# A graph kernel: where in a group its rows and keys are turned, and in what order TensorE and ScalarE take products, turns and counts

## The reference, cut to what matters

```
h = relu(layernorm(x))
m = relu(concat(h[src], edge_attr) @ w1a + b1a) @ w1b + b1b      # one message per edge, 96 wide
agg = segment_sum(m, dst) / max(count, 1)
x = x + (relu(concat(h, agg) @ w2a + b2a) @ w2b + b2b)
f = f0 = relu(layernorm(x))
repeat 10 times:
    f = 0.9 * segment_sum((f * src_norm)[src], dst) * dst_norm + 0.1 * f0
out = x + f
```

## Time and profile before

| what | value |
|---|---|
| median of 3 executions (lowest, highest) | 7052.78 us (7047.1, 7060.38) |
| the profiled execution's own time | 7054.22 us |
| its span | 7052.7 us |
| busy share of the span | PE 80%, PEld 53%, DVE 61%, ACT 10%, POOL 24% |
| mean granted TensorE clock | 0.862 |

### The profile page before, as it was taken

The page is one execution under the profiler, slowest core; times in us unless marked ns, Lnnn a source line. Parts: engine busy times, 40 slices in busy tenths (PEclk is TensorE's granted clock), DMA queues, the critical chain, the costliest instruction groups (busy, mean ns, idle before and its releaser), DMA issues. The chain is left out here.

```text
span 7052.7 us, 211605 instructions
## 1 busy us (share of the span) xinstructions
PE 5638.9 (80%) x85008; PEld 3706.2 (53%) x85008; DVE 4287.4 (61%) x12668; ACT 713.1 (10%) x1695; POOL 1693.6 (24%) x1739
## 2 busy tenths in 40 slices
PE   1455565655555557589999999999999999999998
PEld 1355454544454446446565565656555565656564
DVE  7455555555555557766656666666656666666665
ACT  0122222222222223000000000000000000000000
POOL 5555555555555552500000000000000000000000
PEclk9766666666667667799999999999999999999999
DMA  4322222222222222145555555555555555555554
GB/s 118 76 75 76 75 75 75 75 71 78 73 79 72 75 75 90 37 186 192 200 190 200 190 200 200 190 200 190 200 191 199 191 202 202 187 203 191 199 197 170
DMA packets 442865, 1016.62 MB, mean 144 GB/s; under 512 B 253162, under 2 KB 371914, under 8 KB 387354
## 3 DMA queue, kind: packets, MB, share of 16 engines
q1 hardware_dynamic: 386938, 968.76, 38.8%
q0 software_dynamic: 54944, 33.96, 2.6%
HBM read 838.78 MB, written 176.58 MB: 144 GB/s over the span
## 5 line engine op out<-in xcount | busy, mean ns | idle before, releaser
L1866 PE MATMUL banks_fast<-count_units_fast,feature_parts_fast 128*32 128x512 fp8e3 x70608 | 3826.2, 379 | 31.6 <-DVE count_units_fast L1761 27.0
L1866 PEld LDWEIGHTS banks_fast<-count_units_fast,feature_parts_fast 128*32 128x32 bf16 x70608 | 2154.4, 97 | 1680.2 <-issue 37.4
L1760 DVE TENSOR_SCALAR count_units_fast<-packed_ring_fast 128x512 int32<-128x512 int32 x2949 | 1257.0, 426 | 1427.4 <-PE banks_fast L1866 1396.9
L144 POOL DMA_INDIRECT rows_fast<-row_table,idx_fast x1456 | 1408.6, 967 | 1034.7 <-ACT count_stage_fast L1257 615.7
L1761 DVE TENSOR_SCALAR count_units_fast<-packed_ring_fast 128x512 int32<-128x512 int32 x2949 | 1238.8, 420 | 0.0
L1351 PE MATMUL banks_fast<-w1a_b1a_fast,turn_fast 49*128 49x96 f32 x3136 | 404.4, 399 | 905.1 <-ACT turn_fast L1262 561.4
L1223 DVE TENSOR_SCALAR window_place_hot_fast<-iota_wide_fast,local_keys_fast,target_weight_fast 128x196 bf16<-128x196 f16 x3136 | 939.3, 345 | 0.0
L1351 PEld LDWEIGHTS banks_fast<-w1a_b1a_fast,turn_fast 49*128 49x128 f32 x3136 | 319.6, 281 | 1015.8 <-issue 633.5
L1316 PE MATMUL banks_fast<-window_place_hot_fast,window_src_hot_fast 128*128 128x196 bf16 x3136 | 747.1, 335 | 29.5 <-DVE window_place_hot_fast L1223 25.9
L1322 PE MATMUL banks_fast<-window_place_hot_fast,window_src_hot_fast 128*128 128x196 bf16 x3136 | 728.7, 328 | 6.1 <-issue 6.0
L1219 DVE TENSOR_TENSOR window_src_hot_fast<-iota_by_windows_fast,window_keys_fast 128x1024 bf16<-128x1024 bf16 x392 | 269.6, 688 | 499.1 <-remote 364.1
(11 more groups left out here) (282 smaller groups left out, 1646.7 us busy)
## 6 DMA issues: line engine op xcount, KB each, us to landing
packed_ring_fast<-edge_counts SPq DMA_DIRECT2D x422, 1792.0 KB, 7.0
edge_counts<-count_stage_fast SPq DMA_DIRECT2D x100, 784.0 KB
running_sums<-run_sums_fast SPq DMA_DIRECT2D x100, 768.0 KB
rows_fast<-row_table,idx_fast POOLq DMA_INDIRECT x1456
rows_fast<-attrs_padded SPq DMA_DIRECT2D x98, 128.0 KB
attrs_padded<-in_edge_attr SPq DMA_DIRECT2D x1, 12500.0 KB
rows_fast<-row_table,src_ends_fast POOLq DMA_INDIRECT x112
row_table<-h_nodes_fast SPq DMA_DIRECT2D x1, 1568.0 KB, 5.2
```

Source lines behind the costliest of these rows:

```text
L144: pool.indirect_dma_start(out=self.rows[:, r, c, 0:DN], out_offset=None, in_=b.dram.table, in_offset=bass.IndirectOffsetOnAxis(ap=idx[:, c ...
L1760: nc.vector.tensor_scalar(to[..., 0:P // 8], of, NIBBLES, None, ALU.bitwise_and)
L1866: last = nc.tensor.matmul(b.banks[at:at + DN, SWEEP[m % 2], 0:COLS], parts[:, side, j, k * DN:(k + 1) * DN], of_strip.bitcast(FP8), start= ...
```

## The change

On TensorE the order becomes M0 T1 c0 to c3, M1 T2 c4 to c7, M2 T3 c8 to c11, M3, T0 of the next group, c12 to c15; the very first T0 stands ahead of the loop. On ScalarE it becomes R0 T1 C0 C1, R1 T2 C2 C3, R2 T3 C4 C5, R3, T0 of the next group, C6 C7. The keys of the next pair are turned before M1 of the pair's second group instead of before M3, and ScalarE copies them to SBUF (`kept_keys`) between R1 and the copy of T2; VectorE reads that copy and waits for it in place of R3. The last of the seven passes of the loop is written out behind it on both engines. SyncE's and GpSimd's code is unchanged, and so is the number of matmuls; ScalarE has 50 copies more.

```diff
@@ buffers @@
+        kept_keys = sb("kept_keys", [P, 2 * LW])
+        keys_kept = sem("keys_kept")
...
-        KEYS_AT = 384
+        KEYS_AT, KEYS_TURN = 384, 1
@@ VectorE, pass over the keys of a pair (s == 0) @@
-                        dve.wait_ge(keys_turned, k + 1)
-                        dve.wait_ge(mix_read, g * Q + 1)
+                        dve.wait_ge(keys_kept, k + 1)
                         dve.wait_ge(hot, (SLOTS + g) * WG)
...
-                        part_keys = b.banks[:, M_BANK, KEYS_AT:KEYS_AT + LW]
+                        part_keys = kept_keys[:, 0:LW]
...
-                        nc.vector.scalar_tensor_tensor(out=local[:, :], in0=b.banks[:, M_BANK, KEYS_AT + LW:KEYS_AT + 2 * LW],
+                        nc.vector.scalar_tensor_tensor(out=local[:, :], in0=kept_keys[:, LW:2 * LW],
@@ ScalarE @@
+            def keep_turned(n, slot):
+                act.wait_ge(turned, n + (SLOTS * Q + 1))
+                nc.scalar.copy(turn[:, slot, :], b.banks[:, T_BANK, 0:2 * P]).then_inc(turn_read, 1)
+            def keep_keys(k):
+                act.wait_ge(keys_turned, k + 1)
+                nc.scalar.copy(kept_keys[:, :], b.banks[:, M_BANK, KEYS_AT:KEYS_AT + 2 * LW]).then_inc(keys_kept, 1)
+            keep_keys(0)
+            keep_turned(0, 0)
+            def one_loop(i, last_loop):
...
-                    keep_turned(0)
                     act.wait_ge(sums_out[s], (k + 1) * 16)
                     act.sem_inc(passed, 1)
-                    relu_messages(0)
-                    act.wait_ge(counts_out[s], (k + 1) * 16)
-                    act.sem_inc(passed, 1)
                     for u in range(READS):
+                        q, at = divmod(u, QW // 4)
+                        if at == 0:
+                            relu_messages(q)
+                        if at == 0 and q == KEYS_TURN and s == SLOTS - 1:
+                            act.wait_ge(local_made, (k + 1) * KEY_STEPS)
+                            act.sem_inc(passed, 1)
+                            keep_keys(k + 1)
+                        if at == 0 and not (last_loop and t == BATCH - 1 and q == Q - 1):
+                            keep_turned(g * Q + q + 1, (q + 1) % 2)
+                        if u == 0:
+                            act.wait_ge(counts_out[s], (k + 1) * 16)
+                            act.sem_inc(passed, 1)
                         read_counts(u)
-                        q, at = divmod(u, QW // 4)
-                        if q < Q - 1 and at == 0:
-                            keep_turned(q + 1)
-                        if q < Q - 1 and at == 1:
-                            relu_messages(q + 1)
+            with act.Fori(0, n_loops - 1) as i:
+                one_loop(i, False)
+            one_loop(n_loops - 1, True)
@@ TensorE @@
+            def rows_in(r_rows, turns):
+                pe.wait_ge(gathered[r_rows], (turns + 1) * (G * 16))
+                pe.wait_ge(attrs_in[r_rows], (turns + 1) * 16)
+            def turn_rows(r_rows, q):
...
+            rows_in(0, 0)
+            turn_rows(0, 0)
+            def one_loop(i, last_loop):
...
-                    pe.wait_ge(gathered[r_rows], (turns + 1) * (G * 16))
-                    pe.wait_ge(attrs_in[r_rows], (turns + 1) * 16)
...
                         if q == 0 and s == 0:
-                            pe.wait_ge(local_made, pair * KEY_STEPS + 4)
-                        if q == Q - 1 and s == SLOTS - 1:
+                            pe.wait_ge(keys_kept, pair + 1)
+                        if q == KEYS_TURN + 1 and s == SLOTS - 1:
+                            pe.wait_ge(keys_kept, pair + 2)
+                        if q == KEYS_TURN and s == SLOTS - 1:
...
-                    turn_rows(0)
-                    mix(0)
                     for r in range(WG // 2):
+                        q, at = divmod(r, QW // 2)
+                        if at == 0:
+                            mix(q)
+                        if at == 0 and q < Q - 1:
+                            turn_rows(r_rows, q + 1)
+                        if at == 0 and q == Q - 1 and not (last_loop and t == BATCH - 1):
+                            rows_in((t + 1) % AHEAD_GROUPS, i * (BATCH // AHEAD_GROUPS) + (t + 1) // AHEAD_GROUPS)
+                            turn_rows((t + 1) % AHEAD_GROUPS, 0)
                         count(r)
-                        q, at = divmod(r, QW // 2)
-                        if q < Q - 1 and at == 1:
-                            turn_rows(q + 1)
-                        if q < Q - 1 and at == 2:
-                            mix(q + 1)
+            with pe.Fori(0, n_loops - 1) as i:
+                one_loop(i, False)
+            one_loop(n_loops - 1, True)
```

More of the change, by code:

```diff
@@ L1241, in _ @@
             act.sem_inc(count_read, SLOTS * READS)
-            with act.Fori(0, n_loops) as i:
+            def keep_turned(n, slot):
[7 more added lines that the diff above has]
+            def one_loop(i, last_loop):
                 nc.scalar.activation(first_act[:, :], b.zeros[:, 0:1], ACT.Relu).then_inc(first_done, 1)
@@ L1257, in read_counts @@
                         nc.scalar.copy(to, of).then_inc(count_read, 1)
-                    def keep_turned(q):
-                        act.wait_ge(turned, SLOTS * Q + g * Q + (q + 1))
-                        nc.scalar.copy(turn[:, q % 2, :], b.banks[:, T_BANK, 0:2 * P]).then_inc(turn_read, 1)
                     def relu_messages(q):
@@ L1301, in _ @@
             pe.sem_inc(turned, SLOTS * Q)
-            with pe.Fori(0, n_loops) as i:
+            def rows_in(r_rows, turns):
+                pe.wait_ge(gathered[r_rows], (turns + 1) * (G * 16))
+                pe.wait_ge(attrs_in[r_rows], (turns + 1) * 16)
+            def turn_rows(r_rows, q):
+                for k in range(QC // 2):
+                    c = q * QC + 2 * k
+                    last = nc.tensor.transpose(b.banks[:, T_BANK, k * P:(k + 1) * P],
+                                               rows[:, r_rows, c:c + 2, :].rearrange("p c d -> p (c d)"), b.ident[:, :])
+                last.then_inc(turned, 1)
+            rows_in(0, 0)
+            turn_rows(0, 0)
+            def one_loop(i, last_loop):
                 for t in range(BATCH):
-                    g, pair, s, r_rows, turns = (i * BATCH + t, i * PAIRS_A_LOOP + t // SLOTS, t % SLOTS, t % AHEAD_GROUPS,
-                                                 i * (BATCH // AHEAD_GROUPS) + t // AHEAD_GROUPS)
+                    g, pair, s, r_rows = i * BATCH + t, i * PAIRS_A_LOOP + t // SLOTS, t % SLOTS, t % AHEAD_GROUPS
                     def count(r):
```

## The result

| | before | after |
|---|---|---|
| median of 17 executions each on one chip (lowest, highest) | 7058.65 us (7042.45, 7070.84) | 7034.3 us (7020.29, 7051.65) |
| ratio, 95% interval | | 0.9969 [0.996, 0.9977] |
| profiled execution, its span | 7054.22, 7052.7 us | 7043.64, 7041.5 us |
| mean granted clock | 0.862 | 0.887 |

Faster by 24 us, where 115 were forecast. The time lies in the range (6780 to 7100) and far from the predicted 6940. Two things have to be read: the stage, and what lies behind it.

What follows compares the result with a forecast made beforehand. GpSimd's chain was taken to set the group: 20.5 us floor plus 6.8 us waiting for ScalarE's copies of counts, 27.3. 7054 - 110 (turns ahead) - 5 (last groups) = 6939, say 6940 us; range 6780 to 7100.

Steps and rivals of the forecast that it cites:

- What bounds the kernel: Gather stage: GpSimd's chain sets the 27.3 us group, 20.5 its own floor and 6.8 waiting for ScalarE's copies of counts.
- Turns a quarter ahead, counts in order: TensorE's lead in the gather stage: 1.61 GpSimd stops a group for 2.0, 1.2 us a group over 91 groups, -110 us.
- If T2's late signal arrives before the stop: Optimistic end in the gather stage: M2 and T3 run too, C6 and C7 come in, giving 12.5 DMAs a stop.
- The trickle: TensorE's late signals while gathers are under way, estimated to pass one by one at 0.7 to 1.5 us a signal.
- 8 to 12.5 bounds: Gather DMAs GpSimd issues per stop under the new order; with the ends, 7070 (keys included) and 6857 us.
- The middle, 10.25: DMAs a stop taken between the bounds: 16.5 / 10.25 = 1.61 stops a group, the basis of -110 us.
- Last pass written out: Last loop pass on TensorE and ScalarE: the same instructions in the same number, so 0.
- Signals prompt: Rival: signals are prompt, gathers slow the stage another way; only round trips go, 0.8 x 98 = -77, 6977 us; chance 0.05.
- Keys: Earlier key turns, VectorE's gain worth 0; 50 new ScalarE copies free, or +21 us if all are on the chain.
- ScalarE's order: Rival "slower": C1 and C0 queue behind R and a turn's copy, 0.8 us x 91 = +71, 7125 us; chance 0.19.
- Last groups: Last seven groups, which gather nothing: a turn's round trip, 0.8 us a group, is covered by four counts, -5 us.

## Why the prediction was wrong

**What bounds the kernel: right.** GpSimd's chain sets the group. Its floor of 20.5 us was met within 0.1 where nothing stopped it (20.4), and removing the gathers took 12 us a group off. The late signals are real, and they come at the stops.

**Turns a quarter ahead, counts in order (forecast -110): the failed step.** "If T2's late signal arrives before the stop ... M2 and T3 run too": mostly it does not arrive. The trickle, an estimate of 0.7 to 1.5 us a signal from one place in the earlier trace rows, is slower: nothing came in the 6.73 us before R1, and in the long run of gathers above signals came some 10 and 20 us late. So 8 and 9 DMAs became the usual run, the bottom of the 8 to 12.5 bounds, with some of 10 to 13. The middle, 10.25, had been taken without a row that spoke for it. Counted by the stops for copies of counts, it is 9.2 DMAs a stop where 10.25 were forecast, from 8.0 where 8.25 were read. That is 0.27 stops a group fewer and not 0.39, and each stop is 0.2 us longer, which the sum had at nothing: 2.07 x 3.19 - 1.80 x 3.39 = 0.5 us a group, not 1.2. The whole wait for ScalarE fell by 0.6. Without the loss of propagation this is 47 us of the total (7022.3 to 6975.3), or 24 + 27 = 51 on the chip of the result (38 by its two profiled executions). The order does lengthen the lead, as the prediction said, but by less than half of what it said. Why the stops grew longer is open.

**Last pass written out (forecast 0): the other failed step.** "The same instructions in the same number; 0", and "nothing of the change reaches" propagation. It cost 26 us, shown by removing it and by doing it alone. Of the 115 - 24 = 91 us by which the forecast missed, this is 27, and nearly all of the rest is the turns and counts.

**Signals prompt (0.05):** true of two of the five numbered chips, though not of the one of the result. There the rival's price, -77, was wrong too. GpSimd's floor then sets the group, and the new order is worth 25 us (6388.9 to 6363.9, without the written-out pass), a third of that price.

**Keys (0, at most +21):** within what was said; a small loss is likelier than none. **ScalarE's order (slower, 0.19):** not seen at its price. The stops are 0.2 us longer, not 0.8, and fewer. **Last groups (-5):** right. The last pair takes 30.0 us for 31.2, so 0.6 us a group less, where 0.8 were forecast.

## What to carry to other kernels

Reordering an engine's queue lets it run further ahead only if its signals get out; where they come in bursts, read between which events the bursts lie, and count what is released in one burst, before pricing a longer lead. A loop pass written out is not free: compare the stretches that the change does not touch, and try the same order with the code at its old length. The best version on both kinds of chip is the changed order without the written-out pass: 0.9939 on a late one and 0.9959 on a prompt one, where the changed kernel has 0.9969 to 0.9975 and 1.0005. Four in flight on top of it gave 0.992 on a late chip, which is not clear of 0.9939; on the prompt one it cost 2.7%, the written-out pass among it.

## What the runs showed of the hardware

- TensorE's signals can reach other engines 3 to 20 us late while GpSimd issues indirect DMAs (1.25 us each) without pause, although TensorE works on rows that were gathered some six groups earlier. After a run of 8 DMAs they came 2.6 us after the last was started, after runs of 16 some 4.1 to 4.4 us. With a pause for the landing after each pair they were not held; with no pause and no more than about four in flight they were. What holds them is open.
- In two long runs of gathers (12 and 16 DMAs) TensorE's own matmuls also came one at a time, up to 1.4 us apart, with no wait that the profile names.
- The same program took 6386 to 6389 us on two chips and 7018 to 7059 on the others. On the first two the signals are prompt (0.09 us), with the same gathers at the same 1.25 us a DMA. GpSimd's waits for the copies of counts cost nothing there (1.0005 with and without them), and on a late chip they are worth 6% (1.0613 without them).
- TensorE lost 23 to 28 us in a stage with unchanged instructions when 14 groups of code stood written out before it (4071.9 against 4098.6 us, 4073.5 or 4069.3 against 4096.9), some 6.7 us in each turn of that stage's loop.
